# Soft mixture of experts in steps of two units, with PSUM banks shared in time

## What is computed

```python
def _L1_ffn_ref(x, phi, W, b):
    logits = jnp.einsum('bmd,dnp->bmnp', x, phi)
    dispatch = jax.nn.softmax(logits, axis=0)
    bsz, m, n, p = logits.shape
    combine = jax.nn.softmax(logits.reshape(bsz, m, n * p), axis=-1).reshape(bsz, m, n, p)
    slots = jnp.einsum('bmd,bmnp->bnpd', x, dispatch)
    y = jnp.einsum('bnpd,nde->bnpe', slots, W) + b[None, :, None, :]
    out = jnp.einsum('bnpd,bmnp->bmd', y, combine)
    return out
x = x + _L1_ffn_ref(_layernorm(x, axis=-1), L1_ffn_phi, L1_ffn_W, L1_ffn_b)
```

## Time and profile before

| | us |
|---|---|
| median of 3 runs | 2459.65 (2458.67 to 2463.54) |
| the profiled execution | 2461.69 |
| its span, first to last instruction | 2458.8 |
| PE busy / DVE / ACT / POOL in the span | 2133.5 / 1638.8 / 1564.1 / 1228.4 |
| start of the mixture's block, end of the last DVE operation | 1655.7, 2455.1 |
| mean of one: ACT copy of 128x512, ACT exponential, DVE operation of 128x512, POOL operation | 0.60, 0.64, 0.69, 1.27 |

### The profile page before, as it was taken

The page is one execution under the profiler, slowest core; times in us unless marked ns, Lnnn a source line. Parts: engine busy times, 40 slices in busy tenths (PEclk is TensorE's granted clock), DMA queues, the critical chain, the costliest instruction groups (busy, mean ns, idle before and its releaser), DMA issues. The chain is left out here.

```text
span 2458.8 us, 64346 instructions
## 1 busy us (share of the span) xinstructions
PE 2133.5 (87%) x22522; PEld 1573.4 (64%) x22522; DVE 1638.8 (67%) x4479; ACT 1564.1 (64%) x4481; POOL 1228.4 (50%) x1428
## 2 busy tenths in 40 slices
PE   4999887739999999788968989865599999999999
PEld 2566563326666667455548888863377787778787
DVE  6799749955666666477755555543477767777767
ACT  4677636638887778577747676752766666666652
POOL 4877415428778888667732122210744444444530
PEclk9999955559999999899979999986999999999999
DMA  3000020030000000000000000010000000000101
GB/s 85 2 1 0 2 40 1 0 83 1 1 1 1 0 1 1 10 2 0 1 23 1 1 0 0 0 47 17 3 2 15 15 3 15 15 2 13 47 3 37
DMA packets 49258, 30.31 MB, mean 12 GB/s; under 512 B 21870, under 2 KB 46334, under 8 KB 48894
## 3 DMA queue, kind: packets, MB, share of 16 engines
q1 hardware_dynamic: 39806, 22.98, 3.3%
q10 hardware_dynamic: 9216, 4.20, 0.6%
HBM read 22.97 MB, written 4.19 MB: 11 GB/s over the span
## 5 line engine op out<-in xcount | busy, mean ns | idle before, releaser
L1000 POOL TENSOR_TENSOR ff_hl<-ff_hid,ff_hh 128x512 fp32r<-128x512 f32 x272 | 354.4, 1311 | 111.9 <-ACT ff_hh L1239 105.7
L1845 POOL TENSOR_TENSOR sm_zsum<-sm_zsum,sm_logits 128x512 f32<-128x512 f32 x120 | 155.6, 1296 | 316.3 <-ACT sm_logits L1899 316.3
L525 POOL TENSOR_TENSOR at_kblk<-at_kT,at_heads 128x1024 f32<-128x1024 f32 x128 | 242.2, 1914 | 102.0 <-PE at_p_s L436 92.4
L1168 DVE TENSOR_TENSOR ff_hid<-ff_p_b,ff_hid 128x512 f32<-128x512 f32 x240 | 164.3, 685 | 157.6 <-ACT ff_hid L1228 156.8
L1729 PE MATMUL sm_p_y<-sm_w,sm_sT 128*32 128x128 f32 x8192 | 250.1, 274 | 0.0
L1729 PEld LDWEIGHTS sm_p_y<-sm_w,sm_sT 128*32 128x32 f32 x8192 | 215.8, 110 | 42.3 <-issue 42.3
L1228 ACT ACTIVATE ff_hid<-ff_p_h,ff_b 128x512 f32<-128x512 f32 x272 | 186.0, 684 | 48.5 <-PE ff_p_h L1056 45.5
L1671 PE MATMUL sm_p_l<-sm_phi,g_xnT 128*128 128x256 f32 x512 | 156.5, 431 | 68.5 <-ACT sm_logits L1894 58.2
L1769 DVE TENSOR_REDUCE sm_rmax<-sm_p_l 128x2 f32<-128x512 f32 x128 | 88.5, 691 | 190.5 <-PE sm_p_l L1671 190.4
L1888 ACT ACTIVATE sm_sT<-sm_p_s 128x512 f32<-128x512 f32 x256 | 139.1, 595 | 110.2 <-PE sm_p_s L1713 110.2
L1759 DVE TENSOR_TENSOR sm_yy<-sm_p_y,sm_wb 128x512 f32<-128x512 f32 x256 | 175.7, 691 | 49.7 <-PE sm_p_y L1729 38.2
(11 more groups left out here) (296 smaller groups left out, 5930.7 us busy)
## 6 DMA issues: line engine op xcount, KB each, us to landing
sm_w<-in_w_soft SPq DMA_DIRECT2D x8, 512.0 KB, 3.3
ff_whole<-in_L_ffn_rW SPq DMA_DIRECT2D x30, 128.0 KB, 2.7
early_xs<-in_x ACTq DMA_DIRECT2D x32, 64.0 KB, 1.8
ld_ctx<-in_ctx ACTq DMA_DIRECT2D x32, 64.0 KB, 2.0
ml_vals<-in_ctx SPq DMA_DIRECT2D x8, 256.0 KB, 4.7
x_kept<-early_xs SPq DMA_DIRECT2D x4, 512.0 KB, 3.9
g_xnT<-x_kept SPq DMA_DIRECT2D x1, 2048.0 KB, 9.0
out_x<-sm_acc SPq DMA_DIRECT2D x4, 512.0 KB, 3.2
```

The costliest lines, as they stand in the source:

```text
L525: op = pool.tensor_tensor(kblk[:, v % 2, b, :].rearrange("p (h k) -> p h k", h=NH), row_bc(kT[:, v, b * S:(b + 1) * S], NH), col_bc(heads[ ...
L1000: eng.tensor_tensor(hl[:, q, :], hid[:, q, :], hh[:, q, :].bitcast(F32), ALU.subtract).then_inc(h_split, 1)
L1168: dve.tensor_tensor(h, p_b[e % 2][:, :], h, ALU.mult).then_inc(scaled, 1)
L1845: pool.tensor_tensor(z, z, logits[:, j % RING_L, :, :], ALU.add).then_inc(summed, 1)
```

## The change

Steps are of two units (`pair`), and the leads are in such steps: 64 + 18 steps. PE's order in a step is fold (if any), slots of both units, then logits, transposes, logits, transposes, then experts of both, then outputs of both. So each array shape comes once per step.

Banks: `p_l` gets two, `p_o` two; `p_e` and `p_z` go. The transposes use `p_y[0]` and `p_y[1]`, the fold uses `p_l[1]`, the slots of the odd unit use the two `p_o` banks. That brings waits: the experts wait for the turned copies of both units of the step, the odd slots for the accumulation of the step before, the second logits for the reciprocal in a step with a fold. DVE makes the turned copies of the first 16 units. Per step, ACT's order is exponential, slot copies, turned copy, exponential, turned copy, combine exponentials, logits copies.

The store of x is one DMA in the mixture's block, and the first turned copy and the load back wait for it; `combT` lies where x was. The first two phi loads are issued in the cross attention's block, into a tile that lives throughout. The result is stored in 8 pieces.

```diff
@@ cross_attention, sync
             for dst, src in loads:
                 sync.dma_start(dst, src).then_inc(consts_in, 16)
+            for c in range(2):
+                sync.dma_start(g["phi"][:, c, :], phi_chunks(io)[c]).then_inc(phi_in, 16)
+            sync.wait_ge(phi_in, 32)
@@ soft_experts
-PIECES = 4
+PIECES = 8
-    LEAD_LOGITS, LEAD_COMB, LEAD_TURN, LEAD_NORM, LEAD_SLOTS, LEAD_Y = 36, 20, 19, 3, 2, 1
-    RING_L, RING_C = 35, 20
+    LEAD_LOGITS, LEAD_COMB, LEAD_EXP, LEAD_TURN, LEAD_NORM = 18, 10, 9, 9, 1
+    RING_L, RING_C = 36, 20
...
-        p_l, p_e, p_o, p_z = m.ps("p_l"), m.ps("p_e"), m.ps("p_o"), m.ps("p_z")
+        p_l = [m.ps(f"p_l{i}") for i in range(2)]
         p_s = [m.ps(f"p_s{i}") for i in range(2)]
         p_y = [m.ps(f"p_y{i}") for i in range(2)]
+        p_o = [m.ps(f"p_o{i}") for i in range(2)]
...
+        def pair(i, lead):
+            p = i + lead
+            return (2 * p, 2 * p + 1) if 0 <= p < NU // 2 else ()
...
-                phi_load(0)
-                phi_load(1)
+                sync.dma_start(x_kept[:, :, :], g["xs"][:, :, :]).then_inc(kept, 16)
                 sync.dma_start(fold[:, :], io["c_fold"]).then_inc(fold_in, 16)
@@ tensor, one step
+                    c = fold_of(i)
+                    if c is not None:
...
+                        pe.wait_ge(summed, UNITS * (c + 1))
+                        pe.wait_ge(l_copied, min(2 * (i + LEAD_LOGITS), NU))
+                        for a in range(TU):
+                            mm = pe.matmul(p_l[1][:, 0:CW], fold[:, :], zsum[:, c % 2, a, :], start=a == 0, stop=a == TU - 1)
+                        mm.then_inc(z_done, 1)
+                    for j in pair(i, 0):
+                        bank = (p_s, p_o)[j % 2]
...
+                        if j % 2 == 0:
+                            if j > 0:
+                                pe.wait_ge(s_copied, 2 * (j - 1))
+                        elif j > 1:
+                            pe.wait_ge(acc_made, TU * (j - 1))
+                        pe.wait_ge(normed, j + 1)
...
+                    for h in range(2):
+                        for j in pair(i, LEAD_LOGITS)[h:h + 1]:
...
+                            if j > 1:
+                                pe.wait_ge(l_copied, j - 1)
+                            if h == 1 and fold_of(i) is not None:
+                                pe.wait_ge(rz_made, fold_of(i) + 1)
...
+                        for j in pair(i, LEAD_TURN)[h:h + 1]:
+                            pe.wait_ge(combed, j + 1)
+                            if j > 1:
+                                pe.wait_ge(turn_copied, j - 1)
+                            if i > 0:
+                                pe.wait_ge(y_copied, 4 * min(i, NU // 2))
...
+                    for j in pair(i, 0):
                         c, u = parts(j)
...
                         pe.wait_ge(s_copied, 2 * (j + 1))
+                        pe.wait_ge(turn_copied, min(2 * (i + LEAD_TURN) + 2, NU))
                         for a in range(TU):
                             if j > 0:
                                 pe.wait_ge(y_copied, 2 * (j - 1) + a + 1)
...
+                    for j in pair(i, 0):
                         pe.wait_ge(y_copied, 2 * (j + 1))
@@ vector, one step
+                    for j in pair(i, -1)[1:]:
+                        add_up(j)
...
+                        dve.reciprocal(rz[:, :], p_l[1][:, 0:CW]).then_inc(rz_made, 1)
+                    for j in pair(i, LEAD_NORM):
...
+                    for j in pair(i, LEAD_LOGITS):
...
+                    for j in pair(i, LEAD_TURN):
+                        if j < UNITS:
+                            dve.wait_ge(turned, j + 1)
+                            if j == 0:
+                                dve.wait_ge(kept, 16)
...
+                    for j in pair(i, 0)[:1]:
+                        add_up(j)
@@ gpsimd, one step
+                    for j in pair(i, LEAD_EXP):
...
+                    for j in pair(i, LEAD_COMB):
@@ scalar, one step
+                    for j in pair(i, LEAD_EXP)[:1]:
+                        exp_here(j)
+                    for j in pair(i, 0):
...
+                            act.activation(sT[:, j % 2, :, b, :], (p_s, p_o)[j % 2][b][:, :].rearrange("p (a s) -> p a s", a=TU), ACT.Copy).then_inc(s_copied, 1)
+                    for j in pair(i, LEAD_TURN)[:1]:
+                        turn_copy(j)
+                    for j in pair(i, LEAD_EXP)[1:]:
+                        exp_here(j)
+                    for j in pair(i, LEAD_TURN)[1:]:
+                        turn_copy(j)
...
```

More of the change, by code:

```diff
@@ L1605, in soft_experts, with fold_of @@
         x_back = xnT[:, :].rearrange("p (t d) -> p t d", d=D)
-        def at(i, lead):
-            j = i + lead
-            return j if 0 <= j < NU else None
+        def pair(i, lead):
+            p = i + lead
+            return (2 * p, 2 * p + 1) if 0 <= p < NU // 2 else ()
         def parts(j):
             return j // UNITS, j % UNITS
-        steps = range(-LEAD_LOGITS, NU + 1)
+        def fold_of(i):
+            p = i + LEAD_NORM
+            return p * 2 // UNITS if 0 <= p < NU // 2 and p * 2 % UNITS == 0 else None
+        steps = range(-LEAD_LOGITS, NU // 2 + 1)
         with nc.Block() as block:
@@ L1660, in _ @@
                 for i in steps:
-                    n = i + LEAD_LOGITS
[L1662 to L1672, removed]
+                    c = fold_of(i)
@@ new lines, in _ @@
+                    if c is not None:
+                        if c == 0:
+                            pe.wait_ge(fold_in, 16)
+                        pe.wait_ge(summed, UNITS * (c + 1))
[6 more added lines that the diff above has]
+                        if j == 0:
+                            pe.wait_ge(xt_copied, NT // 4)
+                        if j % 2 == 0:
[4 more added lines that the diff above has]
+                        pe.wait_ge(normed, j + 1)
+                        for a in range(TU):
+                            for b in range(PER):
+                                half = slice(b * S, (b + 1) * S)
+                                mm = pe.matmul(bank[b][:, a * CW:(a + 1) * CW], xn[half, (j % UNITS) * TU + a, :],
+                                               logits[half, j % RING_L, a, :], start=True, stop=True)
+                        mm.then_inc(s_done, 1)
@@ L1673, in _ @@
+                    n = i + LEAD_LOGITS
                     if n < NT // 4:
-                        bank = (p_s + p_y)[n % 4]
+                        bank = (p_s + p_o)[n % 4]
                         if n >= 4:
@@ L1680, in _ @@
                         mm.then_inc(xt_done, 1)
[L1681 to L1705, removed]
-                            pe.wait_ge(xt_copied, NT // 4)
-                        else:
-                            pe.wait_ge(s_copied, 2 * j)
-                        pe.wait_ge(normed, j + 1)
-                        for a in range(TU):
-                            for b in range(PER):
-                                half = slice(b * S, (b + 1) * S)
-                                mm = pe.matmul(p_s[b][:, a * CW:(a + 1) * CW], xn[half, u * TU + a, :],
-                                               logits[half, j % RING_L, a, :], start=True, stop=True)
-                        mm.then_inc(s_done, 1)
-                    j = at(i, LEAD_Y)
-                    if j is not None:
+                    for j in pair(i, 0):
                         c, u = parts(j)
@@ L1913, in program @@
         g["xnT"] = m.sb("xnT", [P, NT * P])
+        g["phi"] = m.sb("phi", [P, 2, CW])
         with Mem(nc, "early") as early:
```

187 lines of the change are left out of this document (85 added, 102 removed).

## The result

The changed kernel takes **2480.76 us** (median of 4 runs, 2476.16 to 2481.65), the kernel before 2461.6 us beside it (4 runs, 2458.67 to 2464.62): ratio 1.0074, 95% interval 1.0055 to 1.0093. It is slower by some 18 us where 25 us less were forecast. The profiled execution took 2480.18 us, its span is 2478.4 us.

A forecast was written before the change was run, and what follows sets the result against it. PE bounds the long part, busy 509.1 of 510.8 us; nothing is busy in chunk 0, POOL busiest in the filling. Terms -6.3 - 44.0 + 8.6 + 11.6 + 0.1 + 1.4 + 4.7 - 1.5 = -25.4 gave 2434.3 us, range 2412 to 2455.

The forecast's parts named there:

- chunk 0, logits only: Mixture's first 8 steps for 16 units: 34.0 us, two steps at half clock and six at full; bounds 31.8 and 47.2.
- filling: From chunk 1's first logits to the first expert block: 54.9 us, POOL without a gap; bounds 54 and 66.
- 45 full steps: Two-unit steps with logits: 11.15 us each, 0.19 slower than two units now, 8.6 us in all; bounds 10.84 and 11.6.
- 9 steps without logits: Steps after the logits end: ACT's copies hold PE, 10.43 us each against 9.14 now, 11.6 us in all.
- Chunk ends: DVE's six small operations now ahead of yy: 1.2 us each, +0.8 over now, six times 4.7 us; bounds 0 and 3 each.
- folded 0.5 us later: In the filling, chunk 0's sum is folded 0.5 us late, since DVE's chain and turned copies hold up the last logits copy.
- A: Rival: loader's gap belongs to each unit's block and stays in all 63 steps, 55 us, total 2489 us; 7%.
- B: Rival: array stays at half clock through chunk 0, 47.2 us instead of 34.0, total 2447.5 us; 15%.
- C: Rival: waits on the shared bank smaller than summed, each 0.5 us per step 31 us, total 2403 us; 12%.
- D: Rival: nothing gained up front, POOL keeps its gap and the clock is low, 2459 us, no change; 5%.
- The first wait: Full steps: expert block waits for both turned copies, sharing p_y; PE stands 0.76 us per step.
- The second: Full steps: unit two's first experts wait for the bank DVE's yy still reads, 0.18 us per step.

The follow-up runs named there:

- the kernel with POOL thin: Changed kernel with POOL's two additions and two centrings touching one column of 256 in chunk-end steps, so not computing the layer: 2443.74 us, ratio 0.9931.
- the chain moved: Changed kernel with DVE's six chunk-end operations moved to the next step, between the normalisations and the logits reductions: 2444.95 us, ratio 0.9931.
- the fold's bank free: Kernel with the six operations moved (2444.95 us), first fold written to a slots bank instead of the second logits bank: 2442.97 us, ratio 0.9932.
- a halved wait: Each expert-block half waits only for its own slot copy, against the reordered kernel waiting for both (2415.03 us): 2394.4 us, ratio 0.9733 to the kernel before.
- another order of PE's and ACT's blocks: Changed kernel with PE's step order transposes, logits, slots, experts, outputs, ACT's turned copies first, fold in a slots bank: 2425.76 us, ratio 0.9855.

## Why the prediction was wrong

Its own case, its sign and its range (2412 to 2455) missed. The sum gave 2436.3 us for an execution like the profiled one; the changed kernel's profiled execution took 2480.18, which is 43.9 more. By step:

| step of the sum | forecast | measured | miss, us |
|---|---|---|---|
| start of the block | 1649.4 | 1650.2 | +0.8 |
| chunk 0, logits only | 34.0 | 34.8 | +0.8 |
| filling | 54.9 | 62.1 | +7.2 |
| 45 full steps, each | 11.15 | 11.31 | +7.2 |
| six chunk ends, each | +1.2 | +3.8 to +5.5 | +22.1, and +2.5 in the steps behind |
| 9 steps without logits, each | 10.43 | 10.61, one 12.08 | +4.0 |
| 9 last steps; steps behind a fold | 7.99 | 8.12 | +1.3; +1.6 |
| experts of the last step to the last output operation; from there to the end | 7.7; as before | 7.85; 2.05 less | -2.0 |

The rest, -1.6, is in no step. The sum was made of differences to the kernel before, and that kernel takes 1.4 us more from its first experts to those of unit 126 than 45, 9 and 9 pairs of its units and its chunk ends and folds add up to; 0.9 of it is that 91 of its units have logits and not 90.

**The failed step is "Chunk ends".** It saw the mechanism (the six operations now stand ahead of yy) and named the row that shows POOL stretching one of them, then took 1.2 us with an upper bound of 3. Of this 0.7 for the chain itself was right (0.70 in the kernel with POOL thin). POOL's part was 3.1 us, not 0.5: POOL does its two centrings and a sum back to back just then, and DVE's operations get through one between each two. The row showed one operation of six lengthened by 1.1 us, and the working counted about half of one such delay, without laying POOL's operations of that moment beside the chain. The Trainium skill (SBUF — State Buffer, "SBUF: two separate sides") has it that a GpSimd operation excludes a DVE operation with two SBUF inputs, or one in a two-port mode such as a float32 copy within SBUF, for a whole instruction. The trace agrees (copies of 0.29 us become 1.27, a maximum of 0.42 becomes 1.37). The prediction gave only the half on two inputs and named two blocked operations by it, some 12 us more, which the sum did not take. Three are blocked at this chunk end (L1814, L1816, L1818), two of them copies, and five in the filling.

**The clock was not in this term at all.** In the step quoted above the half clock added another 2.7 us, so that a wait cost up to 1.7 times itself. Of the 24.6 us that the six chunk ends missed by, POOL and the chain have 15.8 (six times 3.83, the step that kept its clock, less 1.2) and the clock 8.8. Why one of the six waits was spared stays open. No wait of this length was in the long part of the profile before. Its bound should have come from chunk 0, where a logits block was seen at both levels.

**Filling.** POOL itself ran as forecast: its sum of chunk 0 is done 43.4 us after chunk 1's first logits (1728.41 less 1684.96), and the reciprocal follows the fold at the forecast distance. What failed is "folded 0.5 us later": the fold comes at 50.2 us instead of 44.85. The stretched chain (6.8 us) holds the turned copies, these hold PE for 5.0 us, and since the fold shares a bank with the second logits, it waits for their late copy too. The forecast from there to the experts was 10.05 (its terms 1.17, 1.76, 1.5 and 5.56 add to 9.99). The other 1.8 us lies between the first slots and the first experts (7.37 us for 5.56): a wait of 0.83 for a logits copy that was not counted, and one of 1.67 for a turned copy instead of 0.76. With the chain moved the filling is 61.0 us instead of 62.1, with the fold's bank free as well 59.1, and with POOL thin in that step, chain and bank as they were, 57.8. In the last case POOL's own work is shorter too, so 4.3 us is the most that POOL beside the chain can have cost. No run has all of these together.

**Full steps.** The first wait is 0.73 us against 0.76: right. The second is 0.27 against 0.18: the second experts' loads start 1.98 us after the first's (2053.66 - 2051.68), where the forecast had 1.89 and 1.71 without a wait. That is 0.09 of the missing 0.16 us; the rest was not traced to rows. "11.15" as against 10.96 held in sign, the steps did get slower.

**Steps without logits.** Six of the nine take 10.61 to 10.76 us, and one of 11.68 holds a fold. The one of 12.08 has experts partly at the half clock: 128 matmuls in 5.39 us instead of 3.93, behind a wait of only 1.81 us that the others have too.

**Rivals.** A (the gap belongs to the block) has the rows against it: the loader's gaps stand once per step in the changed kernel, and pulling the shapes apart again costs 0.40 us between logits and experts. B did not come: after the first step two more at 5.1 us and then 3.6 us each (logits at 1656.68, 1661.79, 1666.93, then 1670.54, 1674.14). C did not come, the waits were no smaller than summed. D had little gained up front, and the first experts came 41.6 us earlier. Of the signs, the block's start and the place of the first wait came as told. POOL was busy 49.5 of 62.1 us in the filling and not 9.9 of 10, which pointed at the chain. The slow side was covered by A alone, while the mechanism that decided stood in the sum as a term with too narrow bounds.

## What to carry to other kernels

Before an operation chain is put ahead of the work that feeds the bottleneck, lay the other engines' instructions of that same moment beside it: six small DVE operations cost nothing, 0.7 or about 5 us each time by what POOL did and which instruction stood behind them. Where the bottleneck waits, read what it waits for by name and ask whether the work behind needs all of it: here a halved wait and another order of PE's and ACT's blocks, with all instructions the same, were worth some 49 us on top of the moved chain (ratios 0.9931 and 0.9733). And in a pipeline that issues in order, price the queue of every engine on the path, not the operations one by one.

## What the runs showed of the hardware

- With POOL's 1.27 us operations on 128x512 back to back, small DVE operations that read and write SBUF waited for the end of one: 64x256 copies took 1.24 to 1.29 us instead of 0.29, a maximum of 64x256 1.37 to 1.51 instead of 0.42. In the filling this met five of the six; the first, at 1721.78, took its usual 0.18 us, as one of POOL's operations had just ended. DVE operations that read PSUM kept their length beside it: the maximum of 128x512 from the logits bank took 0.68 us at 1721.18 in the changed kernel, under POOL's 2.70 for two from 1720.39.
- A wait of 3.84 to 3.86 us on PE at full clock was followed by the lower level at five of six chunk ends: 64 matmuls in 3.64, 3.30, 3.06, 3.13 and 2.99 us, and 1.95 at the sixth. Waits of 1.81 to 1.96 us, one in each of the nine steps without logits, were followed by it once: 128 matmuls in 5.39 us instead of 3.93, with a mean granted clock of 0.69 (1.00 before and behind).
- A change of the array's shape left the weight loader idle for 0.17 to 0.33 us, and two more of them in a step cost PE 0.40 us between logits and experts (4.15 against 3.75).
